# First scan: the product of gated part and up rows moves from VectorE to POOL, on a copy of the up rows that ACT makes

## What is computed

```
dA  = exp(delta[..., None] * A)               # b l d n, 16 states
dBx = (delta * x)[..., None] * Bm[..., None, :]
h_t = dA_t * h_{t-1} + dBx_t                  # scan over l
y_t = sum over n of h_t * C_t
...
# 16 experts, the best 4 for each token, inner size 176
h   = silu(x @ w_gu.T[:, :176]) * (x @ w_gu.T[:, 176:])
acc = acc + (h @ w_d.T) * weight[:, None]
```

## Time and profile before

| | us |
|---|---|
| median of 3 runs | 1175.77 (1171.88 to 1176.24) |
| profiled execution, its own time | 1175.7 |
| its span, first to last instruction | 1174.0 |
| DVE busy in the span | 902.6 (77%) |
| PE busy | 971.3 (83%) |
| ACT busy | 497.4 (42%) |
| POOL busy | 419.8 (36%) |

### The profile page before, as it was taken

One profiled execution on the slowest core, in us unless ns is written; L12 is line 12 of the kernel. 1 busy time (PEld: TensorE's weight loads), 2 busy tenths in 40 slices (PEclk: granted clock), 3 DMA queues, 4 the chain that ended last, 5 costly groups with the idle time before them and its releaser, 6 DMA issues. The chain is left out here.

```text
span 1174.0 us, 18608 instructions
## 1 busy us (share of the span) xinstructions
PE 971.3 (83%) x6048; PEld 578.1 (49%) x6048; DVE 902.6 (77%) x1508; ACT 497.4 (42%) x1130; POOL 419.8 (36%) x331
## 2 busy tenths in 40 slices
PE   3988998788887878785579877889988999899985
PEld 2354555444444545452444554445655555456553
DVE  4668568899999999999657756767677867776686
ACT  2101125555555555554023135534555545554542
POOL 2000010777788887774100012313322332232310
PEclk9989899999989999987789988979998999899998
DMA  6970080778788888887931123424434443344524
GB/s 217 364 203 1 2 216 23 176 146 164 149 159 154 155 162 156 160 154 125 267 100 51 37 49 84 113 69 105 108 83 93 92 112 88 69 107 97 118 43 144
DMA packets 108657, 144.30 MB, mean 123 GB/s; under 512 B 30789, under 2 KB 98899, under 8 KB 104275
## 3 DMA queue, kind: packets, MB, share of 16 engines
q0 software_dynamic: 30368, 77.92, 34.0%
q1 hardware_dynamic: 78195, 65.18, 20.1%
HBM read 73.72 MB, written 39.58 MB: 97 GB/s over the span
## 5 line engine op out<-in xcount | busy, mean ns | idle before, releaser
L1517 POOL DMA_INDIRECT sum<-yo,to_i x48 | 78.9, 1645 | 306.1 <-ACT yo L1475 285.0
L1185 POOL DMA_INDIRECT xg<-xn_d,token_i x80 | 102.7, 1284 | 176.7 <-DVE to_i L473 93.8
L1178 POOL DMA_INDIRECT sum<-yo,to_i x80 | 138.5, 1731 | 44.2 <-issue 21.4
L1024 PE MATMUL bank<-areaA,xgT 128*128 x320 | 125.6, 519 | 18.9 <-ACT xgT L1079 9.5
L1041 PE MATMUL bank<-areaA,hidT 88*128 x320 | 91.9, 411 | 43.8 <-ACT hidT L1089 42.6
L2101 DVE TENSOR_TENSOR areaD<-areaD,gb 128x512 f32<-128x512 f32 x128 | 87.5, 689 | 49.9 <-ACT areaD L2049 48.9
L1024 PEld LDWEIGHTS bank<-areaA,xgT 128*128 128x128 f32 x320 | 59.9, 205 | 63.8 <-issue 47.7
L1041 PEld LDWEIGHTS bank<-areaA,hidT 88*128 88x128 f32 x320 | 55.1, 192 | 73.2 <-issue 68.8
L1507 POOL DMA_INDIRECT xg<-xn_d,token_i x48 | 53.8, 1120 | 104.4 <-DVE to_i L473 90.1
L699 PE MATMUL bank<-xnT,areaB 128*128 128x512 f32 x192 | 86.8, 599 | 0.8 <-DVE y L729 0.8
L1900 PE MATMUL bank<-xnT,w_in 128*128 128x512 f32 x160 | 83.7, 649 | 1.7 <-ACT ecn L1807 1.2
(11 more groups left out here) (340 smaller groups left out, 2119.5 us busy)
## 6 DMA issues: line engine op xcount, KB each, us to landing
y<-xnT POOLq DMA_DIRECT2D x21, 1024.0 KB, 8.1
wst<-gu_f SPq DMA_DIRECT2D x96, 176.0 KB
y<-areaB POOLq DMA_DIRECT2D x11, 1024.0 KB, 7.4
wst<-down_f SPq DMA_DIRECT2D x48, 176.0 KB
areaA<-in_gu SPq DMA_DIRECT2D x2, 2816.0 KB
gu_f<-in_gu POOLq DMA_DIRECT2D x1, 5632.0 KB, 18.4
sum<-yo SPq DMA_DIRECT2D x2, 2176.0 KB, 16.1
down_f<-in_down POOLq DMA_DIRECT2D x1, 2816.0 KB, 24.6
```

Of the source, the lines that this page charges most:

```text
L1024: last = nc.tensor.matmul(bank[:, GB + q % 2, 0:2 * FI], xgT[:, q % 2, k, :], wgu0_of(e, k), start=(k == 0), stop=(k == KD - 1))
L1178: nc.gpsimd.indirect_dma_start(sum0_d[q % 2], bass.IndirectOffsetOnAxis(ap=to_i[:, q:q + 1], axis=0), yo[:, q % 5, :], None, compute_op=AL ...
L1185: nc.gpsimd.indirect_dma_start(xg[:, q % 5, :], None, xn_d[0], bass.IndirectOffsetOnAxis(ap=token_i[:, q:q + 1], axis=0)).then_inc(s.gathe ...
L1517: nc.gpsimd.indirect_dma_start(sum1_d, bass.IndirectOffsetOnAxis(ap=to_i[:, q:q + 1], axis=0), yo[:, q % 4, :], None, compute_op=ALU.add). ...
```

## The change

The second silu instruction of VectorE is taken out. ACT copies the up columns from PSUM to `hid`, after the tanh of the same tile; VectorE makes the gated part as before and now waits for both of ACT's instructions; POOL multiplies `hid` by the gated part in place. POOL's product stands at the tile's first tick, behind the pair's accumulating DMA where there is one, ahead of the gather. The factor 0.5 goes into the scale of the copy of `hidT`. `tanh_ready` now counts two for each tile; `hid_ready` is raised by POOL. Two waits are new on ACT: the tanh of q waits until POOL has done the product of q - 2, the copy until the transposes of q - 2 are done.

```diff
         def gate_tanh(act, q):
 
             act.wait_ge(s.gu_full, q + 1)
+            if q > 1:
+                act.wait_ge(s.hid_ready, q - 1)
             nc.scalar.activation(act_t[:, q % 2, :], bank[:, GB + q % 2, 0:FI], ACT.Tanh, scale=0.5).then_inc(s.tanh_ready, 1)
+            if q > 1:
+                act.wait_ge(s.hT_full, q - 1)
+            nc.scalar.activation(hid[:, q % 2, :], bank[:, GB + q % 2, FI:2 * FI], ACT.Copy).then_inc(s.tanh_ready, 1)
...
-            nc.scalar.activation(hidT[:, q % 2, :, :], bank[0:FH, HY, 0:2 * P].rearrange("p (k t) -> p k t", k=2), ACT.Copy).then_inc(s.hT_ready, 1)
+            nc.scalar.activation(hidT[:, q % 2, :, :], bank[0:FH, HY, 0:2 * P].rearrange("p (k t) -> p k t", k=2), ACT.Copy, scale=0.5).then_inc(s.hT_ready, 1)
...
         def silu(v, q):
 
-            v.wait_ge(s.tanh_ready, q + 1)
-            first = vec.done(nc.vector.scalar_tensor_tensor(act_t[:, q % 2, :], act_t[:, q % 2, :], 1.0, bank[:, GB + q % 2, 0:FI], ALU.add, ALU.mult))
-            v.wait_ge(vec.sem, first)
-            nc.vector.scalar_tensor_tensor(hid[:, q % 2, :], act_t[:, q % 2, :], 0.5, bank[:, GB + q % 2, FI:2 * FI],
-                                           ALU.mult, ALU.mult).then_inc(s.hid_ready, 1)
+            v.wait_ge(s.tanh_ready, 2 * q + 2)
+            nc.vector.scalar_tensor_tensor(act_t[:, q % 2, :], act_t[:, q % 2, :], 1.0, bank[:, GB + q % 2, 0:FI], ALU.add, ALU.mult).then_inc(gated, 1)
...
+        def times_up(pool, q):
+
+            pool.wait_ge(gated, q + 1)
+            pool.wait_ge(s.tanh_ready, 2 * q + 2)
+            nc.gpsimd.tensor_tensor(hid[:, q % 2, :], hid[:, q % 2, :], act_t[:, q % 2, :], ALU.mult).then_inc(s.hid_ready, 1)
+
...
                 if t and t % (2 * UNIT) == 0:
                     add_scan(pool, t // (2 * UNIT) - 1)
+                if part == 0 and q < NT0:
+                    times_up(pool, q)
                 if part == 0 and q + 6 < NT0:
                     gather(pool, q + 6)
```

More of the change, by code:

```diff
@@ L790, in _program @@
         yT_full, yT_free, x_back = sem("yT_full"), sem("yT_free"), [sem(f"x_back{b}") for b in range(NB)]
-        hc_ready, y_added = sem("hc_ready"), [sem(f"y_added{bp}") for bp in range(2)]
+        gated, hc_ready, y_added = sem("gated"), sem("hc_ready"), [sem(f"y_added{bp}") for bp in range(2)]
         SIDE_UP = {0: 0, 1: 1, 2: 2, 3: 3, 4: 4, 5: 5, 14: 6, 15: 7, 16: 8, 17: 9, 18: 10, 20: 14, 21: 15}
```

## The result

The changed kernel takes 1211.17 us (median of 4 runs, 1208.87 to 1213.41) against 1176.01 us before (median of 4, the three above and one more): a ratio of 1.0277, 95% interval 1.0248 to 1.0307. It is slower by 35 us. The prediction was 1202 us, between 1170 and 1226, with 0.78 on slower.

A forecast was written before the change was run, and what follows sets the result against it. VectorE, 95% busy, bounds the first scan at 4.24 us a tile; with the change POOL would, at 3.89 + 0.50 + 0.08 + 0.15 = 4.62 us. Together +26 us on 1175.7 gives 1202 us, range 1170 to 1226.

The forecast's parts named there:

- POOL's slack of 0.35 us a tile: First scan: POOL needs 3.89 us a tile of the 4.24 a tile takes; the rest is true waiting.
- POOL's time: POOL in the first scan, per tile: 3.89 us needed now, plus 0.50 for the product and 0.08 added blocking.
- with waits 4.62 said: POOL's whole tile in the first scan, with 0.15 us of waits left: 4.62 us against 4.24 now.
- The product: POOL's new 128x176 product of two SBUF operands, per tile: 0.50 us, kept between 0.245 and 0.55.
- Added blocking: POOL's product also waiting while a two-SBUF scan runs: 0.2 us more a scan, 0.08 a tile, at most 0.44.
- signs of being wrong: Profile signs against the forecast: product at 0.3 us or less, fewer blocked POOL gathers, or POOL idle for VectorE's gate.
- the last rival: POOL's product holds two-SBUF scans up to 0.50 us each, VectorE still the bound: 1163 us, chance 0.02.
- 0.38 x 74 - 2: First scan: +0.38 us for 74 tiles with a gather, less 2.2 us for the last six: +26 us together.
- ACT's copy at nothing: ACT's copy of the up columns, 0.32 us a tile, fits ACT's idle time and hides behind TensorE's idle time.
- POOL did not keep up: Rival: POOL's queue absorbs a product of 0.245 us without added blocking or waits, 1166 us; chance 0.09.
- the even case: Rival: POOL's product, blocking and waits make 0.30 to 0.46 us, gain and loss cancel, about 1176 us; chance 0.11.
- The loop through TensorE: Rival: product, transposes, down product, gate_up, tanh, copy and gate set the pace: 4.68 us a tile, up to 5.10; chance 0.10.

The follow-up runs named there:

- work_only: Kernel before plus a 128x176 POOL product of constants into a spare tile that nothing waits for; 1193.89 us, ratio 1.0138.
- work_scan1: Kernel before plus a POOL product on constants nobody waits for, the even units' scan reading its second operand from PSUM; 1176.77 us, ratio 0.9991.
- copy_only: Kernel before plus ACT's copy of the 176 up columns into an unread spare tile, VectorE's silu waiting for it; 1178.84 us, ratio 1.0010.
- mult_first: Changed kernel with POOL's product of q ahead of the scatter of q - 2 and the accumulating DMA; 1211.68 us, ratio 1.0302.
- pass_only: Kernel before with POOL waiting for VectorE's hid and clearing one spare column, TensorE's transposes waiting for that; 1187.83 us, ratio 1.0098.
- half_product: Changed kernel with POOL's product over 88 of the 176 columns, the other half left out; 1201.29 us, ratio 1.0212.
- after_scan1: Changed kernel with the even units' scan reading its second operand from PSUM, so no scan has two SBUF inputs; 1183.64 us, ratio 1.0056.
- gather_first: Changed kernel with POOL's product behind the tile's gather instead of ahead of it; 1247.79 us, ratio 1.0582.

## Why the prediction was right

**What bounds the kernel.** POOL's slack of 0.35 us a tile behind a busy share of 79% was the right reading: `work_only` shows that a product on POOL, 0.52 us net less 0.14 of gap, with nothing else touched, slows the kernel by 16.6 us, and `work_scan1` that it doesn't when 0.42 us of blocking are taken away.

**The terms.** POOL's time: 4.47 us a tile said, 4.43 measured; with waits 4.62 said, 4.61 measured (4.43 and 0.17). The product: 0.50 said, 0.59 net measured, less 0.12 to 0.14 for the shorter gap behind it, which I had not seen coming: 0.45 to 0.47. The product was put too low, the gap and the blocking (below) too high, so that the sum came so close is in part luck; and the measured terms, 3.89 + 0.46 + 0.02, make 4.37 of the 4.43. Slightly longer free gathers and scatters (1.02 against 1.00 us, 1.59 against 1.58) make 0.03 of the rest, what remains is open. With 0.59 us at 176 columns and 0.39 at 88, a column costs 2.2 ns, and some 0.2 us come on top (an estimate from these two). The price in proportion to the 4497 ns for 2048 columns of the Trainium skill's GPSIMD Engine Reference (Elementwise, side-by-side cycle accounting), 0.39 us, was too low, as a proportion has no fixed part; the 2.2 ns a column that it comes to, an estimate from that page, agree with the two products. Added blocking: 0.08 said, about 0.02 measured. I had it wrong in kind: blocking did not grow, it moved from gathers to products. One of my signs of being wrong, blocked gathers becoming fewer, therefore did appear (21 to 2), and the sum stood all the same. A product can hold a scan, too: where one recorded from 354.25 ended at 355.81, the scan that began at 355.38 took 2.59 us and not 2.29. The Trainium skill's SBUF — State Buffer (Who interferes with whom) states that the exclusion holds for GpSimd instructions that read SBUF and that the one that comes first blocks the other. The trace agrees for products; for DMA issues it does not, as in the kernel before the scans that began beside a running scatter or gather took 2.28 to 2.29 us.

```profile
354.25 1.56 POOL L1187 TENSOR_TENSOR hid<-hid,act_t 128x176 f32<-128x176 f32 x1
...
355.38 2.59 DVE L1161 TENSOR_TENSOR_SCAN areaB<-areaB 128x1024 f32<-128x1024 f32 x1
```

That is rare: of 32 such scans five took over 2.35 us, 1.5 us more in all, so the last rival did not decide anything.

**The sum.** 0.38 x 74 - 2 = +26 us said; the stage grew by 27.3 us in the profiled executions, +35 in the medians. Of the 9 us between the forecast and the medians, 1.3 lie in the stage, 5.7 behind it in these two executions, which varies as much between kernels that leave it alone, and 2 are what the medians differ by beyond the profiled executions. Only the first are the forecast's; the others have no cause that a run shows.

**ACT's copy at nothing.** Right, by `copy_only`.

**The rivals.** POOL did not keep up, and the even case failed with it. The loop through TensorE was given 0.10 as the one bound. As the only bound it is refuted by `work_only`, and `mult_first` speaks against it; but it is no slack thing either, as the detour by itself costs 10.5 us (`pass_only`) and 5.2 without blocking, and `half_product` keeps the pace with less work on POOL. Here the prediction's reasoning was wrong: its 4.68 us a tile counts 1.41 us of slack as part of the loop. Without it the parts give 9.35 - 1.41 = 7.94 us for two tiles, 3.97 a tile, far below POOL's 4.62, and by that a bare detour should have cost nothing. `after_scan1` shows what it means: POOL needs 4.1 us a tile there, below the old 4.24, and still none of VectorE's 0.36 us comes through.

**What stays open.** How the 35 us divide between POOL's time and the loop: both stand near 4.6 us a tile in the changed kernel, and runs that relieve one often touch the other. And how much of the loop's part is TensorE's clock: see below; no run held the clock and changed the rest.

## What to carry to other kernels

Before work is moved to an engine with a low busy share, count what that engine needs per step in the stage at hand: dispatch gaps and blocked time belong to its need, waits do not. Then ask who will wait for the moved work and what stands ahead of it in that engine's queue; an operation that took 0.26 us of the engine that set the pace cost 0.6 us here, 2 us and more when a scan held it up, and stood behind a scatter. Test the two apart: the work with nobody waiting, and the wait with hardly any work.

## What the runs showed of the hardware that was not expected

A POOL compute instruction that is queued behind a DMA issue is recorded from before that issue's end (363.99 against 364.42), so its mean of 1335 ns is not its price; ends are. An indirect DMA's gap on POOL is 0.30 us behind another DMA, 0.16 behind a product.

TensorE's granted clock is lower in most kernels whose loop is late: over 250 to 500 us it is 0.95 before, 0.92 in the changed kernel, 0.89 in `mult_first`, 0.87 in `gather_first` and `half_product`. It does not follow the pace strictly: `work_scan1`, as fast as the kernel before, has 0.93. In the changed kernel single tiles' four gate_up matmuls take 2.71 us and not the usual 1.35 to 1.45:

```profile
358.77 1.13 PE L1041 MATMUL bank<-areaA,hidT 88*128 x4 [1.57 <-ACT hidT L1094]
360.26 2.71 PE L1024 MATMUL bank<-areaA,xgT 128*128 x4 [0.37 <-issue]
...
378.59 1.12 PE L1041 MATMUL bank<-areaA,hidT 88*128 x4 [1.28 <-ACT hidT L1094]
...
379.98 1.35 PE L1024 MATMUL bank<-areaA,xgT 128*128 x4
```

In 360.30 to 363.00 the granted clock is 0.50, the level of 1.2 GHz; in 379.98 to 381.30 it is 1.00, 2.4 GHz. Such a fall came after TensorE had waited, here 1.57 us for hidT, but the wait of 1.28 us ahead of 378.59 was followed by none. Of the rows that show a tile's four gate_up matmuls together, 10 take over 2.0 us before, 16 in the changed kernel, 24 in `gather_first`. A slow one adds some 1.3 us (2.71 less 1.38) to a loop that is late already. This was seen and not tested by itself.
